# Values before the turns of x, keys before the last exchange: an order change in a two-layer attention and feed-forward kernel

## The reference, cut to what matters

```python
x = x + fake_quant(layernorm(x)) @ fake_quant(ctx)
# feed-forward, weights quantised in blocks of 32, activations quantised over the whole tensor
xq   = act_qdq(layernorm(x))
up   = act_qdq(xq @ wu.T);  gate = act_qdq(xq @ wg.T)
o    = act_qdq(act_qdq(gate * qdq(sigmoid(gate))) * up)
x = x + o @ wd.T
# cross attention: 32 heads, 8 key heads of 128
q = rmsnorm(layernorm(x) @ wq.T);  k = rmsnorm(ctx @ wk.T);  v = ctx @ wv.T
x = x + softmax(q k^T / sqrt(128) + mask) v @ wo.T
x = x + experts(layernorm(x))          # router and 18 experts
# act_qdq needs the least and the greatest value of its whole argument:
scale = max((mx - mn) / 65535, 1e-12);  zp = clip(round(-mn / scale), 0, 65535)
```

## Time and profile before

| what | us |
|---|---|
| median of three runs | 850.07 |
| lowest and highest of the three | 849.61, 852.84 |
| the profiled execution, its own time | 851.96 |
| its span, first to last instruction | 850.2 |
| around the span (851.96 less 850.2) | 1.8 |

### The profile page before, as it was taken

The page is one execution under the profiler, slowest core; times in us unless marked ns, Lnnn a source line. Parts: engine busy times, 40 slices in busy tenths (PEclk is TensorE's granted clock), DMA queues, the critical chain, the costliest instruction groups (busy, mean ns, idle before and its releaser), DMA issues.

```text
span 850.2 us, 13984 instructions
## 1 busy us (share of the span) xinstructions
PE 780.0 (92%) x4155; PEld 404.7 (48%) x4155; DVE 614.5 (72%) x1343; ACT 534.4 (63%) x996; POOL 462.0 (54%) x482
## 2 busy tenths in 40 slices
PE   0879999857879799999999999999999989999997
PEld 0335544423434455555555555555555565444443
DVE  6997678999846767667676676676676867756665
ACT  4967767797954566666566666666666647455551
POOL 1988657675734555655655655655555243434431
PEclk9999999988979999999999999999999999999999
DMA  8322232100020401311011111011100012232221
GB/s 324 111 88 63 62 93 69 50 1 1 1 100 1 173 0 50 124 51 50 0 49 49 49 49 49 7 43 49 49 0 0 1 39 74 76 111 99 87 74 49
DMA packets 13352, 51.38 MB, mean 60 GB/s; under 512 B 2033, under 2 KB 2289, under 8 KB 10498
## 3 DMA queue, kind: packets, MB, share of 16 engines
q1 hardware_dynamic: 13314, 50.90, 17.4%
HBM read 49.85 MB, written 1.05 MB: 60 GB/s over the span
## 4 chain that ended last, share of the span: by engine, by line
PE 71%; DVE 11%; ACT 6%; issue 6%; POOL 5%; DMA 1%; SPq 0%; DVEq 0%; POOLq 0%; ACTq 0%
PE ps L999 21%; PE ps L1000 20%; PE ps L1001 20%; PE ps L1236 6%; ACT arena L636 4%; DVE arena L1379 3%; DVE arena L1382 2%; PE ps L1206 2%; POOL arena L452 1%; DVE arena L1376 1%; POOL arena L444 1%; ACT arena L704 1%; POOL rk L470 1%; POOL arena L474 1%; PE ps L1051 1%
## 5 line engine op out<-in xcount | busy, mean ns | idle before, releaser
L999 PE MATMUL ps<-arena 128*128 128x512 f16 (+2 forms) x1020 | 383.8, 378 | 17.3 <-ACT arena L636 8.3
L1000 PE MATMUL ps<-arena 128*128 128x512 f16 (+2 forms) x1020 | 383.7, 378 | 0.0
L1001 PE MATMUL ps<-arena 128*128 128x512 f16 (+2 forms) x1020 | 383.2, 377 | 0.0
L636 ACT ACTIVATE arena<-arena 128x512 f16<-128x512 f32 (+11 forms) x270 | 193.7, 735 | 69.6 <-POOL arena L560 28.1
L636 ACT ACTIVATE arena<-ps 128x512 f16<-128x512 f32 (+3 forms) x258 | 146.7, 628 | 112.5 <-PE ps L1001 81.4
L999 PEld LDWEIGHTS ps<-arena 128*128 128x128 f16 (+1 forms) x1020 | 100.7, 99 | 131.4 <-issue 20.1
L586 POOL TENSOR_SCALAR arena<-arena,rden 128x512 f32<-128x512 f32 x128 | 88.6, 692 | 134.2 <-DVE rden L1727 125.4
L1001 PEld LDWEIGHTS ps<-arena 128*128 128x128 f16 (+1 forms) x1020 | 100.8, 99 | 118.3 <-issue 5.8
L1000 PEld LDWEIGHTS ps<-arena 128*128 128x128 f16 (+1 forms) x1020 | 100.8, 99 | 103.9 <-issue 4.7
L1712 DVE CUSTOM_DVE_ANT_0 arena<-ps,arena 128x512 f32<-128x512 f32 x128 | 85.0, 686 | 59.0 <-PE ps L1001 58.7
L1376 DVE TENSOR_TENSOR arena<-ps,arena 128x512 f16<-128x512 f32 x161 | 104.4, 682 | 24.2 <-ACT arena L636 23.8
(11 more groups left out here) (139 smaller groups left out, 763.8 us busy)
## 6 DMA issues: line engine op xcount, KB each, us to landing
arena<-in_moe_w SPq DMA_DIRECT2D x18, 768.0 KB, 4.3
arena<-in_ffn_w SPq DMA_DIRECT2D x33, 256.0 KB, 2.7
arena<-in_wq SPq DMA_DIRECT2D x8, 1024.0 KB, 4.9
arena<-in_wo SPq DMA_DIRECT2D x8, 1024.0 KB, 4.8
arena<-in_kv_w SPq DMA_DIRECT2D x4, 1024.0 KB, 5.0
arena<-in_ctx SPq DMA_DIRECT2D x1, 2048.0 KB, 9.4
arena<-in_ctx_t SPq DMA_DIRECT2D x2, 1024.0 KB, 14.7
arena<-in_x SPq DMA_DIRECT2D x1, 1024.0 KB, 5.0
```

The source lines that it names most:

```text
L636: return a.activation(out_, in_, ACT.Copy, scale=scale, bias=bias)
L999: pe.matmul(out_, lhs[0], rhs[0], start=first, stop=False)
L1000: pe.matmul(out_, lhs[0], rhs[1], start=False, stop=False)
L1001: return pe.matmul(out_, lhs[1], rhs[0], start=False, stop=last)
```

## The change

It moves steps in the program orders and changes no arithmetic. On PE, units 8 and 9 of values move in front of the first weight transposes and the turns of x, and unit 10 takes their place behind the turns; the units 11 to 13 follow the pairs of up tiles, and the last pair has no unit behind it. ACT and POOL follow with `v_out` and `v_low`. In the key stage `k_unit(15)` and the transposes of keys 12 move in front of exchange 4; ACT does `k_square(15)`, `k_high(14)` and `key_out(13)` ahead of the first `out_high`. On DVE the first `k_mean` of the rounds moves in front of round 0, rounds 3 and 7 have none, and `k_mean(15)` becomes the `second` step of `parameters(4)`.

```diff
@@ POOL
-            weights(0)
             v_low(MT + 1)
+            weights(0)
+            v_low(MT + 2)
...
-                v_low(MT + 1 + j)
+                if j < 4:
+                    v_low(MT + 2 + j)
@@ ACT
             x_fraction(0)
+            v_out(7)
             x_fraction(1)
-            v_out(7)
+            v_out(MT)
             x_fraction(2)
             x_fraction(3)
+            v_out(MT + 1)
             weight_high(0)
             hidden_high(0, 1.0)
             weight_high(1)
             round_weights(3)
-            v_out(MT)
-            v_out(MT + 1)
+            v_out(MT + 2)
...
-                if n >= 4 and n % 2 == 0:
-                    v_out(MT + n // 2)
+                if n in (4, 6, 8):
+                    v_out(MT + 1 + n // 2)
...
                 k_high(u)
-                if u + 2 < 2 * MT - 1:
-                    k_square(u + 2)
+                k_square(u + 2)
                 key_out(u - 1)
...
+            k_high(2 * MT - 2)
+            key_out(2 * MT - 3)
             out_high(0)
             out_high(1)
-            k_high(2 * MT - 2)
-            k_square(2 * MT - 1)
             out_high(2)
-            key_out(2 * MT - 3)
             k_high(2 * MT - 1)
@@ PE
-            for u in range(6, MT):
+            for u in range(6, MT + 2):
                 v_unit(u)
             weight_transposes(0)
             weight_transposes(1)
             hidden_transposes(0)
-            v_unit(MT)
-            v_unit(MT + 1)
+            v_unit(MT + 2)
...
-                v_unit(MT + 1 + j)
+                if j < 4:
+                    v_unit(MT + 2 + j)
...
-
-            spread(4)
             k_unit(2 * MT - 1)
             key_transposes(2 * MT - 4)
+
+            spread(4)
             key_transposes(2 * MT - 3)
@@ DVE
             product_int(0)
+            k_mean(5)
+            norms = iter(range(6, 2 * MT - 1))
             for i in range(FT):
                 times_up(i)
                 least(i, p_done)
-                if 5 + i < 2 * MT - 1:
-                    k_mean(5 + i)
+                if i not in (3, 7):
+                    k_mean(next(norms))
                 if i + 1 < FT:
                     product_int(i + 1)
             own.wait(own.n)
-            parameters(4, FT, aqp[:, 3, 7:8])
+            parameters(4, FT, aqp[:, 3, 7:8], None, lambda: k_mean(2 * MT - 1))
...
-                if i == 1:
-                    k_mean(2 * MT - 1)
```

More of the change, by code:

```diff
@@ L504, in _ @@
             v_low(8)
+            v_low(MT + 1)
             weights(0)
-            v_low(MT + 1)
+            v_low(MT + 2)
             for k in range(KD):
```

## The result

The changed kernel takes 849.92 us (median of 20 runs, 847.47 to 851.49). In the same session the kernel before took 851.45 (median of 20), and the ratio is 0.9976, interval 0.9966 to 0.9987: some 2.0 us less, where 2.9 was forecast (one execution of the kernel before, at 2883 us, doesn't move its median). In a second session the ratio was 0.9971. The profiled execution took 848.36 us, its span 846.6 against 850.2. So the two traces differ by 3.6 us, more than the medians do: single executions of one kernel lie up to 5 us apart (849.28 to 854.37 for the kernel before), and most of that goes with the mean granted clock: in one session the kernel before had 0.982 in five runs of 849.3 to 850.5 us and in one of 852.0, 0.980 at 851.2 to 851.7, and 0.976 at 853.3 and 853.5.

A forecast was written before the change was run, and what follows sets the result against it. PE, busy 92% of the span, was taken as the bound, with gains only from its idle time or lower-clock stretches. Part 1's 0.9 plus part 2's 2.0 made 2.9 us: 847.2 us forecast, range 843.8 to 850.8.

The forecast's parts named there:

- the term for the clock at exchange 1: PE's gap of about 3.1 us there brings 3.4 us at half clock: 1.7 us lost, bounds 0 and 3.4.
- The anchor: Profiled execution of 851.96 us taken as 1.9 above the median of 850.07, so 849.1 became 847.2.
- part 1: Values moved at the turns of x: 2.6 - 1.7 = 0.9 us gained, between -0.8 and 2.6.
- The sum of the first tile: After the turns of x, the first up tile starts at 65.8 instead of 68.38, 2.6 us earlier.
- DVE works without a pause there, at the same distance from the tiles: Between last tile and exchange 1: the exchange comes 2.6 us earlier and no more, PE standing about 3.1 before it.
- rival (c): At exchange 1 the lower clock lasts twice as long: 848.9 us; chance 0.08.
- the unit saved in the tiles can't count in full: Up tiles to exchange 1: DVE's chain excludes a further 2.6 us from having one unit fewer in the tiles.
- Part 2: Key stage and norms, to the down product: 1.4 + 0.95 - 0.4 = 2.0 us gained, between 0.3 and 4.3.
- The two holdups: Rounds of keys: a late norm (1.16) and a DVE collision with POOL (1.15) hold ACT up at two places.
- The clock term: First chunk of the down product: half clock the same or up to 3.4 us longer, 0.4 us taken as lost.
- Rival (d): DVE becomes the bound of the rounds, each further collision costing 1.15; slower than before from the third; chance 0.09.
- Rival (a): Rounds of keys: no collision, the norms' lateness small, 2 x 1.15 us more gained: 844.9 us; chance 0.26.

The follow-up runs named there:

- the filled gap: Changed kernel plus one unit of values (12 matmuls) computed again, result unused, on PE in front of exchange 1: ratio 0.9962 to the kernel before.
- the version with the fillings: The version with both repairs plus unused matmuls on PE, 6 in front of exchange 4 and 12 behind it: 840.33 us, ratio 0.9879 to the kernel before.
- the version with both repairs: Changed kernel with unit 13 left in front of exchange 1 and norms one per round as before, keys moved: 844.35 us, ratio 0.9912 to the kernel before.

## Why the forecast was wrong, step by step

Two steps failed: the step from trace to median, and the term for the clock at exchange 1. The mechanism itself came as written down: PE's wait at the turns of x went, the gap in front of exchange 1 brought a stretch at half clock, ACT was held up twice, and `product_int` of rounds 4 and 8 took 1.41.

**The anchor.** The first step that failed is the one from trace to median, "It stood 1.9 above the median of the runs". The 850.07 was a median of three. Over 20 runs the kernel before has 851.45, so its profiled execution stood only 0.5 above; that of after stood 1.6 below its own median. Of the 2.7 us between 847.2 and 849.92 this step is 1.4: the forecast of 2.9 less would have been 848.55 from 851.45. The range from 843.8 to 850.8 held the result, the inner one from 846 to 849 didn't. (From their own terms the ends of the range are 844.0 and 850.65.) By the ratios 2.0 to 2.5 us less were measured, and the 0.4 to 0.9 that is missing is no more than what part 1 failed to give, below.

**Part 1, forecast 0.9, measured 0.2 in the trace and nothing by the ratio.** The sum of the first tile held: 2.5 earlier against 2.6. Exchange 1 came 3.1 earlier (counted from exchange 0) instead of 2.6: "DVE works without a pause there, at the same distance from the tiles" was not right. Before the change DVE began the tile's extremes 1.41 us after ACT's copy, and now 0.72 after it (107.41 to 108.13). In the kernel before, a small step of DVE had met POOL just there and took 1.19 us, where it takes 0.17 in the changed kernel; the two rows of before are

```profile
108.43 1.16 POOL L437 TENSOR_TENSOR arena<-arena 128x512 f16<-128x512 f32 x1
108.43 1.19 DVE L1379 TENSOR_SCALAR dsc<-dsc 128x32 f32<-128x32 f32 x1
```

The half microsecond more is thus luck of the order, and no part of the reasoning. PE's gap was correspondingly shorter, 2.30 and then 0.37, not 3.1.

What failed is the term for the clock: 1.7, taken from exchange 2's gap and its 3.4 us at 0.51. Here the lower clock lasted 6.8 us in three traces and cost 2.9 to 3.1; in a fourth it lasted 3.4 and cost 1.6, as forecast. That is rival (c), to which I gave 0.08. Its size was in the bounds; its chance was too small, as the rows of before already had both lengths, 3.4 at exchange 2 and 6.8 at exchange 4. The lower bound, no loss "where the gap is seen as two short ones", had a row against it too: at the turns of x two gaps of 1.56 and 1.82 were followed by 3.4 us at 0.51.

The sentence that the unit saved in the tiles can't count in full was right for this change and wrong as a rule: the run with unit 13 left where it was gained it. What held it back was where the hole was put.

The Trainium skill (TensorE: Matmul & The Clock Gate, "Why this matters for your kernels") was right to speak against the gap, and the filled gap shows it. It speaks of longer gaps than this one; here 2.30 us were followed by the lower clock in four traces of four.

**Part 2, forecast 2.0, measured 3.65 in the trace.** By the ratios it is less: 1.3 us for the keys and norms without the values (0.2 to 2.4), and about 2 as the whole less part 1. In the trace, by the steps:
- ACT's first round, forecast 207.16, was at 207.31.
- The two holdups were forecast at 1.16 + 1.15 = 2.31 each and measured at 1.84 each (4.97 less 3.13). The collision was there in both places, in rounds 4 and 8, on `product_int`; it cost 0.87 (1.41 less 0.54), not 1.15. The Trainium skill (GPSIMD Engine Reference, "Specifications") has the contention, without a price, for two-input and two-port instructions of DVE; the rows agree that there is one, but whether `product_int`, with its one input, is of the second kind no trace shows. `k_high(13)` was at 236.01 instead of 236.8.
- From there to `out_high(0)` it was 5.73, forecast 5.8.
- The down product started 2.2 earlier, forecast 1.4: most of the difference is the 0.9 that the holdups cost less.
- The wait of 0.95 for keys 14 went, as forecast.
- The clock term had the wrong sign in this trace. I took 0.4 off for a longer stretch over the first chunk; PE had idled 1.65 us in front of the transposes of keys 13, the lower clock had started at 239.2 already, and was over before the chunk's end: 0.5 gained. In the trace of the keys and norms without the values, with the same steps around this place, the chunk took 5.08 instead of 4.44: 0.6 lost. So this term isn't fixed by the order alone.

Together 2.2 + 0.95 + 0.5 = 3.65. Rival (d) fell: no third collision in the rounds. (There was one right behind them, `out_int(1)` with 1.38 us beside a `k_low`; it moved DVE's `out_low(0)`, which ACT releases, by less than 0.1.) Rival (a) fell by its condition, since the collision came.

The price of the collision could have been read from the kernel before, from the same kind of instruction (L1379, 128x512, float to integer) beside a POOL step of the gate stage:

```profile
177.01 1.04 POOL L444 TENSOR_TENSOR arena<-arena,dsi 128x512 f32<-128x512 f32 x1
177.00 1.34 DVE L1379 TENSOR_SCALAR arena<-arena,aqp 128x512 int32<-128x512 f32 x1
```

It ended 0.29 after POOL's. The two that met a `k_low` of 1.15 after 0.02 to 0.03 us also ended 0.29 after it: 1.15 - 0.03 + 0.29 = 1.41.

Why the medians show only about 2 of the 3.65 is settled in part. At the same mean granted clock the changed kernel is 2.4 to 3.1 us faster. In the second session the mean times, before and after, were 849.85 and 846.92 at 0.982, 851.86 and 848.74 at 0.980, 852.89 and 850.12 at 0.978, 854.43 and 852.08 at 0.976 (one, three, seven and one executions of the changed kernel). But it was at 0.980 or above in only 4 of 12 executions, the kernel before in 24 of 34. The second trace of the changed kernel shows such a case: it takes 600.2 us from the transposes of keys 14 to the end instead of 599.4, and has one more stretch of lower clock there, from 290.9 to 294.4. Why these stretches are more frequent in the changed kernel stays open.

## What to carry to other kernels

Look where the hole goes, not only how large it is. A unit of filler work belongs where the engine would otherwise wait for an exchange, and the work that is taken away should come from a place that the engine itself paces: the same units of values gained nothing in one order and some 4 us in the other. In front of an exchange that can't be moved, useless matmuls cost 0.1 us here (61.31 against 61.19) and kept the clock up. A collision of DVE and POOL is best priced from a row with the same DVE instruction, by how long after POOL's it ended. Before a forecast is anchored on a median, ask how far single runs lie apart; here three runs of the kernel before missed its median by 1.4 us, half of what was to be forecast.

## What the runs showed of the hardware

- The same gap of PE (2.30 us, 0.37 us behind it) was followed by 6.8 us at half clock in three executions and by 3.4 us in a fourth. The eight other traces have at most 0.40 us of idling in front of that exchange, and no lower clock behind it. The wait of 2.0 us in front of exchange 2 was followed by 3.4 us of it in ten of the twelve traces, by 6.8 in one and by none in one. PE's wait of 1.57 us in front of the down product, in the version with the fillings, was followed by none. So the length isn't told by the gap alone.
- A `TENSOR_SCALAR` of DVE from SBUF to SBUF took 1.41 instead of 0.54 us when it ran beside POOL's `TENSOR_TENSOR` of 1.15, and ended 0.29 us after it. The two-input one of the earlier trace rows ended 0.55 after POOL's. A `TENSOR_SCALAR` on only 128x32 took 1.19 instead of 0.17 beside one of 1.16, and ended 0.03 after it. A `TENSOR_REDUCE` wholly inside such a one kept its 0.69.
- With 18 matmuls whose results nobody reads, the version with both repairs went from a ratio of 0.9912 to one of 0.9879, about 3 us; the two were measured on different chips and their intervals touch. Within the traces the first chunk of the down product became 2.4 us shorter.
